# Seven products instead of eight for the down projection in the first pass, and a list schedule with new durations and ranks

## The reference

```
q, k, v = x @ wq, x @ wk, x @ wv             # 32 query heads, 8 key/value heads of 32
q, k = rope(q), rope(k)
attn = softmax(q k^T / sqrt(32) + causal mask)
x1 = layernorm(x + (attn v) @ wo)
gate, up, down = gate_t * gate_s, up_t * up_s, down_t * down_s    # gate_t, up_t, down_t: int32 of -1, 0, 1; 3584 hidden columns
hidden = silu(x1 @ gate.T) * (x1 @ up.T)
out = layernorm(x1 + hidden @ down.T)
```

## Time and profile before

| | |
|---|---|
| median of 3 runs | 1801.59 us (1798.89 to 1803.57) |
| the profiled execution's own time | 1802.76 us |
| its span, first to last instruction | 1801.0 us |
| TensorE busy, share of the span | 1747.7 us, 97% |
| VectorE | 1167.2 us, 65% |
| ScalarE | 830.0 us, 46% |
| GpSimd | 458.9 us, 25% |
| granted TensorE clock, mean | 0.997 |
| last attention product of TensorE ends, about | 697 us |
| second pass begins, about | 1221 us |

### The profile page before, as it was taken

How to read it: one execution, slowest core, us unless ns; L and a number is a source line. 1 busy time by engine, 2 the same in 40 slices (tenths; PEclk the granted TensorE clock), 3 DMA queues, 4 the chain that set the end, 5 groups by cost and what they waited for, 6 DMA issues and landing times.

```text
span 1801.0 us, 27008 instructions
## 1 busy us (share of the span) xinstructions
PE 1747.7 (97%) x9840; PEld 849.8 (47%) x9840; DVE 1167.2 (65%) x2423; ACT 830.0 (46%) x1675; POOL 458.9 (25%) x813
## 2 busy tenths in 40 slices
PE   7999999999899999999999999999999999999998
PEld 4744564464455433444444444444444444444444
DVE  7897688488758755556454445646656666677456
ACT  6686668467546655266243343341332232231321
POOL 3364446454454553310000001202100000003103
PEclk9999999999999999999999999999999999999999
DMA  9564344234334697477635435558411121122302
GB/s 262 104 136 84 72 128 115 60 101 130 55 76 130 152 207 259 166 257 266 207 124 174 138 134 191 181 161 190 143 62 65 45 81 64 62 108 88 111 12 82
DMA packets 228852, 233.47 MB, mean 130 GB/s; under 512 B 184048, under 2 KB 184688, under 8 KB 228720
## 3 DMA queue, kind: packets, MB, share of 16 engines
q1 hardware_dynamic: 227856, 231.26, 44.1%
q10 hardware_dynamic: 864, 0.49, 0.1%
HBM read 122.78 MB, written 72.88 MB: 109 GB/s over the span
## 4 chain that ended last, share of the span: by engine, by line
PE 82%; DVE 8%; DMA 3%; issue 2%; SPq 2%; ACT 1%; POOL 1%; DVEq 0%; ACTq 0%; POOLq 0%
PE bank L1202 37%; PE bank L1086 16%; PE bank L1222 14%; PE bank L1235 6%; PE bank L1128 3%; PE bank L1102 3%; PE bank L1146 3%; DVE bank L1453 1%; DMA q_stack<-max_rows 1%; SPq L1767 1%; DMA x_forms<-x_forms_spill 1%; PE bank L1161 1%; SPq L1824 1%; DMA att_parts<-att_spill 1%; DMA x_forms_spill<-x_parts 0%
## 5 line engine op out<-in xcount | busy, mean ns | idle before, releaser
L1202 PE MATMUL bank<-x_forms,weight_forms 128*128 128x512 f16 x3136 | 698.1, 379 | 4.1 <-DVE up_blocks L1615 1.6
L1202 PEld LDWEIGHTS bank<-x_forms,weight_forms 128*128 128x128 f16 x3136 | 306.2, 98 | 376.4 <-DVE up_blocks L1615 4.2
L1222 PE MATMUL bank<-down_forms 128*128 128x512 f16 (+1 forms) x1168 | 256.3, 376 | 0.0
L1294 ACT ACTIVATE p_tiles<-bank 128x512 f32<-128x512 f32 (+1 forms) x352 | 184.4, 566 | 73.1 <-PE bank L1128 68.9
L1720 POOL TENSOR_TENSOR acc<-acc,down_forms 128x1024 f32<-128x1024 f32 x16 | 39.1, 2454 | 696.9 <-DVE acc L1650 696.9
L1086 PE MATMUL bank<-wq_parts,xT_parts 128*128 128x256 f16 x1536 | 204.1, 275 | 8.5 <-DVE wq_parts L1409 8.0
L1453 DVE CUSTOM_DVE_ANT_0 bank<-bank,cmask 128x512 f32<-128x512 f32 (+2 forms) x320 | 179.8, 607 | 44.8 <-PE bank L1102 44.3
L1650 DVE TENSOR_TENSOR acc<-bank,acc 128x512 f32<-128x512 f32 x188 | 128.5, 689 | 103.3 <-PE bank L1222 64.9
L1222 PEld LDWEIGHTS bank<-down_forms 128*128 128x128 f16 x1168 | 114.3, 98 | 134.6
L1086 PEld LDWEIGHTS bank<-wq_parts,xT_parts 128*128 128x128 f16 x1536 | 150.1, 98 | 55.9 <-DVE wq_parts L1409 8.0
L1086 PE MATMUL bank<-wo_parts,att_parts 128*128 128x512 f16 x672 | 163.5, 384 | 3.6 <-DMA att_parts<-att_spill 3.3
(11 more groups left out here) (136 smaller groups left out, 2073.7 us busy)
## 6 DMA issues: line engine op xcount, KB each, us to landing
weight_forms_spill<-weight_forms SPq DMA_DIRECT2D x28, 896.0 KB, 4.7
weight_forms<-weight_forms_spill SPq DMA_DIRECT2D x28, 896.0 KB, 4.6
x_forms_spill<-x_parts SPq DMA_DIRECT2D x56, 256.0 KB, 2.6
w_page<-gateT SPq DMA_DIRECT2D x28, 512.0 KB, 5.3
w_page<-upT SPq DMA_DIRECT2D x28, 512.0 KB, 4.1
w_page<-downT SPq DMA_DIRECT2D x28, 512.0 KB, 3.6
att_spill<-att_made SPq DMA_DIRECT2D x64, 128.0 KB, 2.2
down_forms<-x_spill SPq DMA_DIRECT2D x16, 512.0 KB, 3.5
```

What stands on the lines that cost most here:

```text
L1202: t = nc.tensor.matmul(strassen[bank_set(use)][to][:, :], w_form[:, use % 4, A_FORMS[a_form], k * P:(k + 1) * P], xF[:, :, B_FORMS[b_form] ...
L1222: t = nc.tensor.matmul(to[:, 0:cols.stop - cols.start], hid_p[place_of(r)][:, k, a, i // 2 * P:(i // 2 + 1) * P], wd_p[place_of(r)][:, c, ...
L1294: nc.scalar.activation(p32[j][:, h0:h0 + heads, :], bank[5 + m % 2][:, 0:heads * n].rearrange("p (h c) -> p h c", c=n), ACT.Exp, scale=SCO ...
```

## The change

It does three things.

1. `plain(n)` now is true only for the last four rounds of a pass, so that ten rounds of the first pass use the seven products too. The down weights are cast straight into the first four slots of `down_forms` (`down_rows`), and VectorE makes `T1`, `T2`, `T4`, `T3`, `T3` last, since it overwrites a slot that `d_store` reads. `T2` is made from other operands. The ring has three places for these rounds, so a round may be written when the down products of the round three before it are done.
2. The durations in the plan, the time that a result takes to another engine (`HOP`, now one per engine) and the times of transfers have new numbers, and `AT_ONCE` lists pairs of pieces on one engine between which that time counts too.
3. `SHIFTS` has new numbers throughout.

```diff
-HOP = .15
-TAIL = .12
-LANDS = 1.9
-FIRST_MOVES, PAGE_MOVES, FORM_MOVES, TURN_MOVES, FORMS_MOVE = 1.3, 1.85, .95, 1.31, 3.3
+HOP = {"PE": .2, "ACT": .155, "DVE": .16, "POOL": .2, "SP": 0.0}
+LANDS, ISSUES = 1.75, .05
+FIRST_MOVES, PAGE_MOVES, STORE_MOVES, FORM_MOVES, TURN_MOVES, FORMS_MOVE = 1.3, 1.85, .9, .75, 1.31, 2.85
...
-DOWN_MADE = ["T1", "T3", "T2", "T4"]
+DOWN_MADE = ["T1", "T2", "T4", "T3"]
...
-DOWNS = [(q, m) for q in range(PASSES * ND) for m in range(PAIRS * NPR if ND <= q < PASSES * ND - 1 else 2 * PT)]
+DOWNS = [(q, m) for q in range(PASSES * ND) for m in range(PAIRS * NPR if q % ND < ND - 1 else 2 * PT)]
...
 def plain(n):
 
-    return n < NF or n % NF >= PLAIN
+    return n % NF >= PLAIN
...
 def room_after(n):
 
     p, r = divmod(n, NF)
-    if p == 0:
-        return DOWN_OF[r - 4] if r > 3 else None
-    return DOWN_OF[p * NF + min(r - 3, PLAIN - 1)] if r > 2 else p * ND - 1
+    if r > 2:
+        return DOWN_OF[p * NF + min(r - 3, PLAIN - 1)]
+    return p * ND - 1 if p else None
...
 SHIFTS = {
-    PE: {"down": -9, "max_tr": 2, "product": 4, "proj_out": -20, "proj_q": 54, "pv": 19, "sums": -1},
...
+    PE: {"down": 11, "max_tr": 10, "product": 200, "proj_out": -2, "proj_q": 12, "pv": -7, "score_k": 1, "score_q": 5,
+         "sums": -134},
...
+AT_ONCE = {("sum", "hidden"), ("hidden", "hid_form"), ("hid_form", "hid_form"), ("ln_step", "max_parts"), ("d_form", "d_form"), ("sum_turn", "att_scale"),
+           ("residual", "norm_stats"), ("acc", "norm_stats"), ("x1_form", "x1_form"), ("ln_seed", "ln_step")}
...
-        put(SY, end + 2, .4, "max_rows", u, moves=.1, after=[("max_copy", u)] + (
+        put(SY, end + 2, 2.0, "max_rows", u, moves=.1, after=[("max_copy", u)] + (
...
-            for _ in range(4 if n < NF else 10):
+            for _ in range(10):
                 if left and DOWN_ROUNDS[left[0][0]][-1] < n:
                     down_at[left.pop(0)] = clock
-                    clock += one if n < NF else one / 2
+                    clock += one / 2
...
-            put(VE, at + one / (1 if plain(rounds[0]) else 2), .72, "acc", q, m, after=[("down", q, m)] + room)
+            put(VE, at + one / (1 if plain(rounds[0]) else 2), .61, "acc", q, m, after=[("down", q, m)] + room)
...
         if w == 2 and c == 1:
             put(SY, at + 6, .4, "d_store", r, moves=PAGE_MOVES, after=[("w_cast", w, r, 0), ("w_cast", w, r, 1)])
+            for k, form in enumerate(DOWN_MADE * (not plain(r))):
+                put(VE, at + 8 + .5 * k, .45, "d_form", r, form, after=[("w_cast", w, r, 0), ("w_cast", w, r, 1)] + (
+                    [("d_form", r, DOWN_MADE[k - 1])] if k else []) + ([("d_store", r)] if form == "T3" else []))
...
+        def down_rows(n):
+
+            return wd_p[place_of(n)].rearrange("p c d -> p (c d)") if plain(n) else wd_f[n % NF % 3][:, 0:4, :].rearrange("p f c -> p (f c)")
...
-                                           "T2": (5, 1, 0, ALU.add), "T4": (6, 2, 5, ALU.subtract)}[form]
+                                           "T2": (5, 3, 4, ALU.subtract), "T4": (6, 2, 5, ALU.subtract)}[form]
```

More of the change, by code:

```diff
@@ L239 @@
 SHIFTS = {
-    PE: {"down": -9, "max_tr": 2, "product": 4, "proj_out": -20, "proj_q": 54, "pv": 19, "sums": -1},
-    SC: {"att_hi": 9, "copy": -15, "exp": 18, "hid_hi": 15, "ln_exp": 11, "nat_hi": 150, "norm": -6, "row_sum": 128, "silu": 13,
-         "split_hi": 138, "v_copy": -8, "w_cast": 82, "x1_hi": 60},
-    VE: {"acc": -10, "add_x1": -8, "att_lo": -16, "att_scale": -14, "bound": 30, "d_form": 11, "ds_scale": 15, "hid_form": -40,
-         "hid_lo": -32, "hidden": 256, "ln_seed": 17, "ln_step": 34, "max_copy": -17, "max_parts": 80, "residual": 36,
-         "rotate": -4, "row_max": 25, "split_lo": 19, "sum": -43, "sum_turn": 17, "w_form": -44, "x1_lo": -32},
@@ new lines @@
+    SC: {"att_hi": 11, "copy": -77, "exp": 122, "hid_hi": -61, "ln_exp": -7, "nat_hi": 135, "norm": 30, "row_sum": 4, "silu": 68,
+         "split_hi": 77, "v_copy": -37, "w_cast": 291, "x1_hi": -12},
+    VE: {"acc": -90, "add_x1": 10, "att_lo": -17, "att_scale": 40, "bound": -35, "d_form": -1, "ds_scale": -15, "hid_form": 9,
+         "hid_lo": 90, "hidden": -65, "ln_seed": -172, "ln_step": -4, "max_copy": -30, "max_parts": -12, "norm_stats": -124,
+         "residual": 3, "rotate": -68, "row_max": -12, "split_lo": -26, "sum": -5, "w_form": 77, "x1_lo": 10},
@@ L622, in ffn_plan @@
             before = [("copy", n, w, i - 1)] if i else [("copy", *divmod(use - 1, 2), 2)] if use else []
-            put(SC, at, .6, "copy", n, w, i, after=[ended(use, (1, 2, 3)[i])] + before + (old[i] if n else attention))
+            put(SC, at, .5, "copy", n, w, i, after=[ended(use, (1, 2, 3)[i])] + before + (old[i] if n else attention))
         for k in range(3):
@@ L626, in ffn_plan @@
             before = [("sum", n, w, k - 1)] if k else [("sum", *divmod(use - 1, 2), 2)] if use else []
[L627 removed]
+            put(VE, at - 4, .61, "sum", n, w, k, after=[("copy", n, w, (0, 2, 2)[k]), ended(use, (0, 4, 5)[k])] + before)
         for k in range(4):
```

137 lines of the change are left out of this document (73 added, 64 removed).

## The result

The changed kernel takes 1790.29 us (median of 4 runs, 1788.83 to 1791.56) beside 1801.79 us for the kernel before (4 runs): ratio 0.9937, 95% interval 0.9922 to 0.9952. It is faster by 11.5 us where 27 were forecast, and the time lies just above the predicted range of 1759 to 1790.

The account below looks back on a forecast made before the run. TensorE, busy 97% of the span, was taken as the bound. Terms -17.3 + 3 - 6.7 - 2.5 - 2.0 - 1.5 + 0 = -27.0 us gave 1774 us in the median's terms, range 1759 to 1790.

Parts of the forecast that it names:

- Matmuls removed: First pass, TensorE: five changed groups lose 80 matmuls of 512 columns at 0.216 us each, -17.3 us.
- Work added on VectorE: First pass: VectorE's load rises to 77%, so TensorE waits more for `acc`; +3 us, bounds 0 and 10.
- The second pass: Second feed-forward pass: same work as before, products and down products alternating a little more strictly; costed at nothing.
- maxima: Attention: more matmuls between `max_tr` and `score_k` cover TensorE's wait for `max_rows`; -6.7 us, bounds -7.7 and 0.
- exponentials: Attention's last unit: output matmuls now lie between scores that waited for `exp`; -2.5 us, bounds -2.9 and 0.
- loads: Attention rows: load waits change as an output tile more is held back as filler; -1.5 us, bounds -3.3 and +3.
- the chain before `max_tr`: Attention: 8.7 us of waits before `max_tr` taken as unchanged, 0 us; bounds -8.7 and +9.
- The first products: Feed-forward's start: an output tile in front covers waits for weight forms and a block sum; -2.0 us, bounds -2.1 and 0.
- The ring of three places: First pass: weights wait for the ring place of three rounds before instead of four, covered by a round's length; costed at nothing.
- A: Whole kernel: only the matmuls go, and the new order has as many waits at other places; 1787 us, chance 0.20.
- C: Attention: every unit's `max_parts` on VectorE meets a long GpSimd addition; +24 us, 1798 us, chance 0.04.
- D: First pass: VectorE's fixed order delays one `acc` in each of 70 turns, 42 us; slower, 1813 us, chance 0.04.

Follow-up runs that it names:

- after_again: The changed kernel, unaltered, run and profiled a second time: 1788.56 us, ratio 0.9928 to the kernel before.
- scale_short: The changed kernel with GpSimd's `scale_row` multiplication by `down_s` cut to one column instead of 1024: 1779.20 us, ratio 0.9875 to the kernel before.
- sums_first: scale_dve with a set's weight sums allowed only behind the first block sum of the set before: 1779.46 us, ratio 0.9893 to the kernel before.
- scale_dve: The changed kernel with the `scale_row` multiplications by `down_s` moved from GpSimd to VectorE: 1782.52 us, ratio 0.9898 to the kernel before.
- seven_only: The kernel before with seven products in the first pass's ten rounds, old durations and ranks kept: 1799.53 us, ratio 0.9994 to the kernel before.

## Why the prediction failed

- **Matmuls removed, -17.3: right.** 80 fewer, at 0.216 us in both traces.
- **Work added on VectorE, +3 with bounds 0 and 10: the step that failed.** The load was right (78% for 77%), but on equal work the first pass gained 7.6 us and not 14.3, so the term measured 17.3 - 7.6 = +9.7 in this profile and +7.2 in after_again's. I took the price from the second pass as the nearest row and left `scale_row` out, which hardly met VectorE in the first pass before. scale_short, with the same order, has 6.7 us less in this stretch (4.2 against after_again), so the meeting accounts for half of the term or more. The rest goes with waits for block sums and weight sums, 2.9 us in scale_short where the kernel before has 1.1; no run on this kernel tested it, for the wait that sums_first takes away is one of scale_dve's own. Of the 9.7, idle time is 7.6. Another 2.0 hide in the way a matmul's end is modelled: there are 12 waits more, and in front of each the last matmul counts as busy for 0.16 us beyond the start that a next one would have had.
- **The second pass, 0: wrong, +3.7 in this profile and +1.8 in after_again's.** I wrote that it "has the same work as before, with down products and products taking turns a little more strictly". By the rows the turns fell so that two held instructions came in a row, 2.10 us of wait and 1.7 of lower clock. I had not priced the clock at all, though in this execution it made the wait nearly twice as dear.
- **Attention, -10.7 for maxima, exponentials and loads: near in sum only.** Idle time fell 8.4, and the clock, which I had no term for, gave some 1.7 more: it fell at two places of this stretch before (416.7 and 631.8 us) and at one now (614.8). But `max_rows` gave 3.0 (6.7 forecast; one wait of 2.9 us is left), the exponentials 1.2 (2.5), the loads +0.3 (-1.5), while the chain before `max_tr`, taken as 0, gave 6.8, and 4.3 us of waits for GpSimd's tiles are new: L1720 2.5 and 1.0, L1728 0.8. I was right for partly wrong reasons.
- **The first products, -2.0: wrong, about +0.4.** They waited 2.1 us and wait 0.52 (at 693.54) + 0.69 (at 696.12) + 1.27 (at 763.29) = 2.5 us now. An output tile in front of them did not help. The whole way into the feed-forward idles 1.8 us more; its longest wait is one that no term had, 1.69 us at 735.95, where an output tile waits for VectorE's `row` (L1539).
- **The ring of three places at no cost: right for the pair, wrong for the edit.** With the old ranks it cost, by the rows, 5.4 us and a clock drop in one place (seven_only).
- **The rivals.** A ("only the matmuls go", 1787 us) came nearest. It is closest to the truth in size but not in kind: attention's waits did go, and the feed-forward took as much back. C had the right mechanism at the wrong place: I argued from GpSimd's 14.10 of 305 us that it was rarely busy there, and didn't ask what stands behind the instructions that it would hold. D did not happen: the first pass has 4.9 us of waits for `acc`, not 42.

## What to carry to other kernels

Before a stage is changed, ask of every long instruction on another engine what it could hold, and what stands behind that in the new order: GpSimd's 16 multiplications, half of which had scarcely met VectorE before, cost 11 of the 15.5 us that the gain fell short. Here a short GpSimd job with two SBUF operands was better on VectorE, even one that is 70% busy, since the results behind it feed TensorE. And a change of structure and a change of order must be judged as a pair: here each alone gave nothing or a loss, and together they gave 11.5 us.
